# A fused two-layer attention kernel: the preparation stage is dissolved into the start of the key side

## The chip, the cores and the metric

The kernel runs on one core of one Trainium2 chip. The metric is the device time of one execution in microseconds, the median of three runs. A core has TensorE (PE: matmuls and transpositions, results in PSUM), VectorE (DVE), ScalarE (ACT), GpSimd (POOL) and SyncE (SP), which here issues DMAs. Each engine works through its own list of instructions in order; semaphores hold an engine until another has got far enough.

## The reference

Two layers work on `x` (32 batches, 64 rows, 512 columns) with a context of the same shape. Layer 0 is an attention with eight heads and a feed forward with ternary weights. Layer 1 is a linear attention and a gated low-rank projection. The parts that matter here:

```python
# layer 0 attention: 64x64 weights and biases
q = _proj(Wq, bq, x_query); k = _proj(Wk, bk, x_key); v = _proj(Wv, bv, x_value)
...
return _proj(Wo, bo, x)
# layer 1 attention: Wq, Wk, Wv are 512x64, Wo is 64x512
kh = jnp.einsum('bcn,oc->bon', k, Wk).reshape(b, HEADS, DIM_HEAD, -1)
vh = jnp.einsum('bcn,oc->bon', v, Wv).reshape(b, HEADS, DIM_HEAD, -1)
kh = jax.nn.softmax(kh, axis=-1)
context = jnp.einsum('bhdn,bhen->bhde', kh, vh)
out = jnp.einsum('bhde,bhdn->bhen', context, qh)
out = jnp.einsum('bcn,oc->bon', out, Wo) + bo[None, :, None]
```

`kh` and `vh` of layer 1 come from the context input alone. So the kernel computes the product of keys and context for all batches first, with `Wv` and `Wo` of each head multiplied into one matrix, and keeps it as `M`.

## The kernel before

The program is a chain of blocks, in the order of `program`: `prepare`, `key_side`, `attention0`, `feed_forward`, `query_side`, `projection`, `experts`. All engines meet at the end of each block, so nothing of a block starts before the one ahead of it is finished on every engine.

`prepare` makes what later blocks need of small weights and constants. SP loads the key weights of layer 1 twice side by side (`wdup`, so that both halves of the partitions hold them), the first context tile (`cf0`), `wv1` and `wo1`, the query weights, the second context tile and the first three pieces of the feed forward's weights. ScalarE issues 14 loads: two biases, four 64x64 weights in two copies, and `bv`, `bo` in two copies. Then it loads its table of functions. TensorE turns (transposes) the key weights into PSUM. ScalarE copies them in half precision (`wk_hi`) and DVE subtracts this copy (`wk_lo`), so that two halves carry the accuracy of one float. The same is done with the query weights. `Wo1` is turned and copied (`wo1T`), multiplied with `wv1` head by head, and scaled into `wv_wo`. The four small weights are turned and copied into `wT0` for layer 0. The biases are split into three rows of short floats (`biases`).

`key_side` works on 16 tiles of 128 rows (two batches each), four chunks of 128 key columns to a tile. For each tile GpSimd makes `cs_hi` (`high`) and DVE `cs_lo` (`low`) from `cf`. For each chunk TensorE makes the keys in one of two PSUM buffers (`keys`, six matmuls), DVE takes the maximum of a row (`keys_max`), and ScalarE two exponentials with their sums (`exponentials`). With all four chunks of a tile done, TensorE turns them back (`turn`, into `psT`), ScalarE and DVE copy them (`eT`), TensorE multiplies them with the turned context (`gather`, into `psG`) and with `wv_wo` (`matrix`, into `psM`), and DVE writes `M`. TensorE is written one tile ahead: it makes the keys of tile t+1 between the turns of tile t, so five keys groups (tile 0 and the first chunk of tile 1) stand before the loop. This start is the "ramp" below.

Beside this the weights of the feed forward pass twice through a ring of three buffers. In tiles 0 to 6 they are summed (`magnitudes`), then DVE makes `winv` (`scales`), and from tile 7 on GpSimd rounds them (`ternary`) and SP sends them through transposing DMAs (`turn` on SP). SP's loads wait for counts of tiles or of sums. The order of each engine is the order in which the code issues; no scheduler changes it.

## Time and profile before

| | us |
|---|---|
| median of 3 runs | 810.43 (809.3 to 810.54) |
| the profiled execution | 810.15 |
| its span in the profile | 808.3 |
| TensorE busy | 687.0 (85%) |
| VectorE busy | 621.2 (77%) |
| ScalarE busy | 483.1 (60%) |
| GpSimd busy | 364.2 (45%) |

The busy shares are means over stages with different limits. The preparation stage lies in the first 19 us; the key side goes on to about 233 us. A row of the timeline gives the start, the duration, the engine, the line of the kernel, the operation with what it writes and reads, and how many of its kind are merged in it. In square brackets stands how long the engine had been idle before it, and what released it. "issue" there is time in which the engine waited for nothing that the profile shows. SPq and ACTq are the issuing of DMAs by SP and ScalarE. The granted clock is the share of TensorE's full 2.4 GHz.

### The profile page before, as it was taken

The numbers are of one execution on the slowest core, as the hardware profiler recorded it, in microseconds if no ns is written. First come the engines' busy times: TensorE is split into PE (matmuls) and PEld (weight loads), VectorE is DVE, ScalarE is ACT, GpSimd is POOL, SyncE is SP. The second block draws the span as 40 slices with busy tenths as digits, with TensorE's granted clock in tenths as the row PEclk, the third lists the DMA queues.
The fourth block names the chain that finished last, engine by engine and source line by source line (L and its number), as shares of the span: only waits on it lengthen the run. The fifth ranks groups of instructions, "written<-read, shape, count | busy, mean of one in ns | idle before, by whom it ended". The sixth has DMA issues, their size and how long they took to land. (4 is left out here: it accounts for less than half of the span.)

```text
span 808.3 us, 17679 instructions
## 1 busy us (share of the span) xinstructions
PE 687.0 (85%) x6606; PEld 357.8 (44%) x6633; DVE 621.2 (77%) x1028; ACT 483.1 (60%) x873; POOL 364.2 (45%) x271
## 2 busy tenths in 40 slices
PE   2799999999977767499999479999999999479944
PEld 1345454554545555244444134444444444145541
DVE  4687788888636667499998579999999999355456
ACT  1687867667525657277777247787878787422100
POOL 1000008999925664022212146767777776343100
PEclk9999999999999999599999969999999999879955
DMA  5043555555442331023343100000000000035305
GB/s 149 27 136 111 200 186 147 157 147 154 89 126 77 72 82 30 15 56 74 74 71 70 37 0 1 2 2 0 2 1 2 2 1 1 1 72 85 53 2 208
DMA packets 94504, 54.98 MB, mean 68 GB/s; under 512 B 78868, under 2 KB 78868, under 8 KB 94420
## 3 DMA queue, kind: packets, MB, share of 16 engines
q1 hardware_dynamic: 93456, 53.71, 26.5%
q8 instruction: 54, 0.88, 0.4%
q10 hardware_dynamic: 964, 0.13, 0.1%
q14 instruction: 30, 0.25, 0.1%
HBM read 32.27 MB, written 4.19 MB: 45 GB/s over the span
## 5 line engine op out<-in xcount | busy, mean ns | idle before, releaser
L1314 POOL TENSOR_TENSOR query_qn<-query_eq,query_rq 128x1024 f32<-128x1024 f32 x64 | 121.7, 1902 | 56.6 <-DVE query_rq L1248 54.7
L610 ACT ACTIVATE keys_ek<-keys_psK,keys_mk 128x512 f32<-128x512 f32 x128 | 86.8, 684 | 39.8 <-DVE keys_mk L524 38.1
L524 DVE TENSOR_REDUCE keys_mk<-keys_psK 128x2 f32<-128x1024 f32 x64 | 77.9, 1217 | 22.5 <-PE keys_psK L662 21.7
L1239 DVE TENSOR_REDUCE query_mq<-query_psQ 128x16 bf16<-128x1024 f32 x64 | 75.6, 1181 | 5.0 <-PE query_psQ L1382 4.8
L1245 DVE TENSOR_REDUCE query_lq<-query_eq 128x16 f32<-128x1024 f32 x64 | 77.2, 1207 | 2.6 <-ACT query_eq L1323 2.5
L1323 ACT ACTIVATE query_eq<-query_psQ 128x1024 f32<-128x1024 f32 x64 | 65.2, 1018 | 22.6 <-PE query_psQ L1395 22.6
L1404 PE MATMUL query_psX<-all_ident,query_qn 128*128 128x128 f32 x512 | 70.4, 281 | 0.0
L673 PE MATMUL keys_psT<-all_ident,keys_ek 128*128 128x128 f32 x512 | 70.1, 280 | 0.0
L685 PE MATMUL keys_psG<-keys_eT,keys_cT 128*64 128x512 f32 x256 | 69.0, 617 | 1.0 <-issue 0.9
L1042 POOL TENSOR_SCALAR ff_hr<-ff_h,ff_qs 128x1376 f32<-128x1376 f32 x16 | 22.6, 1412 | 104.5 <-DVE ff_qs L1089 104.5
L673 PEld LDWEIGHTS keys_psT<-all_ident,keys_ek 128*128 128x128 f32 x512 | 54.8, 141 | 27.9 <-issue 21.3
L1330 ACT ACTIVATE query_qT<-query_psX 128x1024 f32<-128x1024 f32 x64 | 65.4, 1022 | 0.9 <-PE query_psX L1404 0.9
L1414 PE MATMUL query_psF<-query_qT,all_M 128*64 128x512 f32 x256 | 61.8, 604 | 1.1 <-ACT query_qT L1330 1.1
L1404 PEld LDWEIGHTS query_psX<-all_ident,query_qn 128*128 128x128 f32 x512 | 55.3, 142 | 15.7 <-issue 14.3
L499 POOL TENSOR_SCALAR keys_st<-all_ring 128x1024 bf16<-128x1024 f32 (+2 forms) x16 | 60.7, 3795 | 1.3
L487 POOL TENSOR_SCALAR keys_cs_hi<-all_cf 128x512 f16<-128x512 f32 x16 | 9.9, 618 | 106.8 <-DMA all_cf<-in_ctx_dram 82.4
L529 DVE COPY keys_eT<-keys_psT 128x512 f32<-128x512 f32 x80 | 53.1, 680 | 2.6 <-PE keys_psT L673 2.3
L1163 PE MATMUL ff_psG<-all_wgT,ff_xT 128*128 128x512 bf16 (+1 forms) x190 | 45.9, 364 | 10.1 <-DMA ff_xT<-ff_xq 10.1
L1136 ACT ACTIVATE ff_r<-ff_psG,all_sg 128x512 f32<-128x512 f32 (+1 forms) x48 | 30.8, 642 | 35.7 <-PE ff_psG L1163 34.0
L1537 PE MATMUL proj_psH<-all_ring,proj_x_T 128*128 128x512 f16 x192 | 46.1, 392 | 0.0
L1177 PE MATMUL ff_psD<-all_wdT,ff_hT 128*128 128x512 bf16 (+1 forms) x171 | 39.6, 379 | 7.0 <-DMA ff_hT<-ff_hq 6.8
L1168 PE MATMUL ff_psU<-all_wuT,ff_xT 128*128 128x512 bf16 (+1 forms) x188 | 45.0, 362 | 0.2
(243 smaller groups left out, 1436.3 us busy)
## 6 DMA issues: line engine op xcount, KB each, us to landing
all_ring<-in_L_ffn_w_down_dram SPq DMA_DIRECT2D x8, 688.0 KB, 4.3
all_ring<-in_L_ffn_w_gate_dram SPq DMA_DIRECT2D x10, 512.0 KB, 6.6
all_ring<-in_L_ffn_w_up_dram SPq DMA_DIRECT2D x10, 512.0 KB, 3.7
all_cf<-in_ctx_dram SPq DMA_DIRECT2D x16, 256.0 KB, 2.7
all_x_res<-in_x_dram SPq DMA_DIRECT2D x4, 1024.0 KB, 6.2
att_ctx_n<-in_ctx_dram SPq DMA_DIRECT2D x16, 256.0 KB, 3.2
out_dram<-all_x_res SPq DMA_DIRECT2D x16, 256.0 KB, 2.2
att_w_nat<-in_L_ffn_W_dram SPq DMA_DIRECT2D x4, 256.0 KB, 4.2
```

The source lines that it names most:

```text
L499: pool.tensor_scalar(st[v % 2][:, 0:w], r, -ROUND, 0.0, ALU.add, ALU.add).then_inc(cast_ok, 1)
L524: dve.tensor_reduce(mk[:, c, :], psK[c % 2][:, :, :], X, ALU.max, negate=True).then_inc(mk_ok, 1)
L610: act.activation(ek[t % 2][b][:, c, :], psK[c % 2][:, b, :], ACT.Exp, bias=mk[:, c, b:b + 1], accum_out=le[t % 2][:, b, c:c + 1]).then_inc ...
L673: mm = pe.transpose(chunk(psT[b], c), chunk(ek[t % 2][b][:, c, :], j), k.ident[:, :])
L685: mm = pe.matmul(psG[HALF[b], :], cT[t % 2][:, j, b * D:(b + 1) * D], eT[b][:, j, :], start=j == 0, stop=j == NC - 1)
L1239: dve.tensor_reduce(mq[g % 2][:, :, 0:HEADS], psQ[g % 2][:, :, :].rearrange("p b (h d) -> p b h d", d=D), X, ALU.max, negate=True).then_in ...
L1245: dve.tensor_reduce(lq[:, :], eq[g % 3][:, :, :], X, ALU.add).then_inc(lq_ok, 1)
L1314: pool.tensor_tensor(qn[m % 2][:, :, :], eq[m % 3][:, :, :], rq[m % 2][:, :].unsqueeze(2).broadcast_to([P, 2 * HEADS, D]), ALU.mult).then_ ...
L1323: act.activation(eq[g % 3][:, :, :].rearrange("p h d -> p (h d)"), psQ[g % 2][:, :, :].rearrange("p b n -> p (b n)"), ACT.Exp).then_inc(eq ...
L1330: act.activation(qT[t % 2][:, :, c * P:(c + 1) * P], psX[:, :, :].rearrange("p b (j n) -> p (b j) n", n=P), ACT.Copy).then_inc(qT_ok, 1)
L1404: mm = pe.transpose(psX[:, b, j * P:(j + 1) * P], qn[g % 2][:, b * HEADS + 2 * j:b * HEADS + 2 * j + 2, :].rearrange("p h d -> p (h d)"), ...
L1414: mm = pe.matmul(psF[HALF[b], :], k.M[:, 2 * t + b, j, :], qT[t % 2][:, b * NC + j, :], start=j == 0, stop=j == NC - 1)
```

## The change

`prepare` and its block are gone. Its work is written into the lists of `key_side`, with a semaphore where there was a barrier.

- Loads. ScalarE issues only `cf0`, `wv1` and `wo1` and loads its table. SP issues the key weights, `cf1`, the four small weights (once each), the query weights, the biases and the first ring pieces. `bv` and `bo` are loaded by SP at tile 2.
- TensorE turns the key weights and `Wo1`, then makes the keys of chunks 0 and 1. The small weights, the query weights and the product of `wv1` and `wo1T` follow between the next keys groups.
- DVE makes `wk_lo` and both `cs_lo`, and then, between the maxima of tile 0, `wq_hi` (before on ScalarE), `wq_lo`, `wT0` (before on ScalarE) and `wv_wo`. The biases follow in three portions in tiles 1 to 3.
- Buffers. `wdup` lies in `eT1`; the PSUM results lie in `psT0`, `psT1` and `psG`, which are free until the first turn. The other small buffers belong to the key side.

```diff
+        wdup = eT[1][:, 0:2, :].rearrange("p m (c d) -> p m c d", c=NC)
...
@@ key_side, SP
+            for h in range(2):
+                sp.dma_start(wdup[:, 1, :, h * D:(h + 1) * D], a["Wk1"].rearrange("(c p) d -> p c d", p=P)).then_inc(wk_in, 16)
+            sp.dma_start(cf[1][:, :], nat[1]).then_inc(c_in[1], 16)
+            for n, w in enumerate((a["Wq0"], a["Wk0"], a["Wv0"], a["Wo0"])):
+                sp.dma_start(w_two[:, n, :], w).then_inc(two_in, 16)
+            for h in range(2):
+                sp.dma_start(wdup[:, 0, :, h * D:(h + 1) * D], a["Wq1"].rearrange("(c p) d -> p c d", p=P)).then_inc(wq_in, 16)
...
+                if t == 2:
+                    for h in range(2):
+                        sp.dma_start(k.bv2[HALF[h], :], a["bv0"].unsqueeze(1)).then_inc(two_in, 16)
+                        sp.dma_start(k.bo2[HALF[h], :], a["bo0"].unsqueeze(1)).then_inc(two_in, 16)
@@ key_side, VectorE
+            dve.wait_ge(wkhi_ok, 1)
+            dve.tensor_tensor(k.wk_lo[:, :], psT[0][:, :], k.wk_hi[:, :], ALU.subtract).then_inc(w_ok, 1)
             low(0)
+            dve.wait_ge(w_ps, O_TURNED)
+            dve.tensor_copy(wo1T[:, :, :], psG[:, 0:NC * D].rearrange("p (n m) -> p n m", n=NC)).then_inc(w_ok, 1)
             low(1)
-            for c in range(NC + 1):
-                keys_max(c // NC, c % NC)
...
             for t in range(TILES + 1):
...
+                    if c == 0 and 1 <= t < 4:
+                        biases(t - 1)
@@ key_side, ScalarE
+            act.dma_start(cf[0][:, :], nat[0]).then_inc(c_in[0], 16)
+            act.dma_start(wv1[:, :, :], a["Wv1"].rearrange("(c p) d -> p c d", p=P)).then_inc(vo_in, 16)
+            act.dma_start(wo1[:, :], a["Wo1"]).then_inc(vo_in, 16)
+            act.preload_act_table_set("natural_log_exp_and_others")
+            act.wait_ge(w_ps, K_TURNED)
+            act.activation(k.wk_hi[:, :], psT[0][:, :], ACT.Copy).then_inc(wkhi_ok, 1)
+            act.wait_ge(const_ok, CONSTS)
@@ key_side, TensorE
+            turned_keys()
+            turned_output()
+            pe.wait_ge(w_ok, WK_OK)
+            keys(0, 0)
+            keys(0, 1)
+            context(0)
+            turned_two()
+            turned_queries()
+            keys(0, 2)
+            product()
+            keys(0, 3)
+            pe.wait_ge(const_ok, CONSTS)
+            keys(1, 0)
+            pe.wait_ge(w_ok, VO_OK)
@@ program
-                    prepare(nc, a, k)
                     key_side(nc, a, k)
```

What the change moves on VectorE, at the start of the program. Before, its list runs from the first use of the turned key weights (`wk_lo`) through the whole preparation to the first maxima:

```order
L229 TENSOR_TENSOR all_wk_lo<-prep_psK,all_wk_hi 128x512 [waits prep_hi_ok]
L231 COPY prep_wo1T<-prep_psO 128x256 [waits prep_t_ps]
L233 TENSOR_TENSOR all_wq_lo<-prep_psQ,all_wq_hi 128x512 [waits prep_hi_ok]
L202 CAST prep_part<-prep_brow 1x128 [waits all_b_in]
...
L239 TENSOR_SCALAR all_wv_wo<-prep_psV 64x4x64 [waits prep_zero_ok,prep_t_ps]
L239 TENSOR_SCALAR all_wv_wo<-prep_psV 64x4x64 x3
L120 UNCONDITIONAL_BRANCH
L514 UNCONDITIONAL_BRANCH [waits barrier_Pool_Activation_PE_DVE_SP_release]
L519 TENSOR_TENSOR keys_cs_lo<-all_cf,keys_cs_hi 128x512 [waits keys_hi_ok] x2
L524 TENSOR_REDUCE keys_mk<-keys_psK 128x2 [waits keys_k_ps] x4
```

In the changed kernel the same engine has, from `wk_lo` on:

```order
L492 TENSOR_TENSOR all_wk_lo<-keys_psT,all_wk_hi 128x512 [waits keys_wkhi_ok]
L406 TENSOR_TENSOR keys_cs_lo<-all_cf,keys_cs_hi 128x512 [waits keys_hi_ok]
L495 COPY keys_wo1T<-keys_psG 128x256 [waits keys_w_ps]
L406 TENSOR_TENSOR keys_cs_lo<-all_cf,keys_cs_hi 128x512 [waits keys_hi_ok]
L411 TENSOR_REDUCE keys_mk<-keys_psK 128x2 [waits keys_k_ps] x2
L500 CAST all_wq_hi<-keys_psT 128x512 [waits keys_w_ps]
L502 TENSOR_TENSOR all_wq_lo<-keys_psT,all_wq_hi 128x512 [waits keys_wkhi_ok]
L411 TENSOR_REDUCE keys_mk<-keys_psK 128x2 [waits keys_k_ps]
L505 COPY all_wT<-keys_psT 64x256 x2
L411 TENSOR_REDUCE keys_mk<-keys_psK 128x2 [waits keys_k_ps]
L511 TENSOR_SCALAR all_wv_wo<-keys_psG 64x4x64 [waits keys_zero_ok,keys_w_ps]
```

The maxima (`keys_mk`) stood behind all of the preparation; now query weights, small weights and product stand between them, and the bias instructions are no longer here.

On TensorE, before, the five parts of the preparation stand ahead of the block's end and of the first keys:

```order
L248 MATMUL prep_psK<-all_ident,prep_wdup 128x128 [waits prep_k_in,prep_ident_ok]
...
L252 MATMUL prep_psO<-all_ident,prep_wo 128x64 [waits prep_vo_in]
...
L256 MATMUL prep_psQ<-all_ident,prep_wdup 128x128 [waits prep_q_in]
...
L260 MATMUL prep_psW<-all_ident,prep_w_two 64x128 [waits prep_two_in]
...
L265 MATMUL prep_psV<-prep_wo1T,prep_wv 64x64 [waits prep_oT_ok]
...
L645 UNCONDITIONAL_BRANCH [waits barrier_Pool_Activation_PE_DVE_SP_release]
L662 MATMUL keys_psK<-keys_cs_hi,all_wk_hi 128x512 [waits keys_lo_ok]
```

Now TensorE's list begins so; `keys_w_two` are the small weights, `keys_eT` holds the key and later the query weights:

```order
L657 MATMUL keys_psT<-all_ident,keys_eT 128x128 [waits keys_wk_in,keys_ident_ok]
...
L663 MATMUL keys_psG<-all_ident,keys_wo 128x64 [waits keys_vo_in]
...
L617 MATMUL keys_psK<-keys_cs_hi,all_wk_hi 128x512 [waits keys_lo_ok,keys_w_ok]
...
L617 MATMUL keys_psK<-keys_cs_hi,all_wk_hi 128x512 [waits keys_lo_ok]
...
L669 MATMUL keys_psT<-all_ident,keys_w_two 64x64 [waits keys_two_in]
...
L675 MATMUL keys_psT<-all_ident,keys_eT 128x128 [waits keys_wq_in]
...
L617 MATMUL keys_psK<-keys_cs_hi,all_wk_hi 128x512 [waits keys_ek_ok,keys_lo_ok]
...
L682 MATMUL keys_psG<-keys_wo1T,keys_wv 64x64 [waits keys_w_ok]
```

Two parts are left ahead of the first keys; the small weights and the query weights stand behind the second keys group, and the product behind the third.

## Rows read from the trace of the kernel before

**Rows 1.** Busy time of each engine in two stretches, granted clock, DMA share, GB/s

```profile
10.00:20.00 10.00, 2.11 (x20) 1.47 (x20) 5.30 (x18) 2.81 (x5) 0.66 (x2) 1.00 0.31 111
140.00:160.00 20.00, 20.00 (x151) 10.18 (x149) 17.30 (x26) 12.45 (x31) 19.50 (x13) 1.00 0.54 141
```

**Rows 2.** Timeline to 21 us: start, duration, engine, line, operation, count, idle before

```profile
0.72 1.00 SPq L142 DMA_DIRECT2D prep_wdup<-in_L_xattn_Wk_dram  x2
...
4.44 1.09 PE L248 MATMUL prep_psK<-all_ident,prep_wdup 128*128 128x128 f32 x4 [4.44 <-DMA prep_wdup<-in_L_xattn_Wk_dram]
...
6.95 0.69 PE L252 MATMUL prep_psO<-all_ident,prep_wo 64*128 64x64 f32 x4 [1.42 <-DMA prep_wo<-in_L_xattn_Wo_dram]
...
7.99 1.12 PE L256 MATMUL prep_psQ<-all_ident,prep_wdup 128*128 128x128 f32 x4 [0.36 <-DMA prep_wdup<-in_L_xattn_Wq_dram]
...
9.69 1.28 ACT L163 ACT_TABLE_LOAD   x1 [9.69 <-issue]
10.98 0.60 ACT L165 ACTIVATE all_wk_hi<-prep_psK 128x512 f16<-128x512 f32 x1
...
11.61 0.69 DVE L229 TENSOR_TENSOR all_wk_lo<-prep_psK,all_wk_hi 128x512 f16<-128x512 f32 x1 [7.23 <-ACT all_wk_hi L165]
...
13.15 0.20 DVE L202 CAST prep_part<-prep_brow 1x128 bf16<-1x128 f32 x1
...
14.92 0.49 DVE L209 CAST all_bias_rows<-prep_rest 1x256 bf16<-1x256 f32 x2
...
15.02 1.06 PE L260 MATMUL prep_psW<-all_ident,prep_w_two 128*64 128x128 f32 x4 [5.91 <-DMA all_bo<-in_L_xattn_bo_dram]
...
17.18 1.76 DVE L239 TENSOR_SCALAR all_wv_wo<-prep_psV 64x256 f32<-64x256 f32 x4 [1.77 <-PE prep_psV L265]
19.34 1.20 POOL L487 TENSOR_SCALAR keys_cs_hi<-all_cf 128x512 f16<-128x512 f32 x2 [15.92 <-POOLq L120]
...
21.14 0.61 PE L662 MATMUL keys_psK<-keys_cs_hi,all_wk_hi 64*128 64x512 f16 x2 [4.01 <-DVE keys_cs_lo L519]
```

**Rows 3.** Groups by line and shape up to 19.3 us, VectorE: busy, mean ns, idle

```profile
L231 DVE COPY prep_wo1T<-prep_psO 128x256 f32<-128x256 f32 x1 | 0.4, 411 | 0.0
```

**Rows 4.** Busy time in the third microsecond, columns as rows 1

```profile
2.00:3.00 1.00, 0.00 (x0) 0.00 (x0) 0.44 (x1) 0.00 (x0) 1.00 (x2) 1.00 0.95 211
```

**Rows 5.** Groups by line from 24 to 34 us, VectorE

```profile
L524 DVE TENSOR_REDUCE keys_mk<-keys_psK 128x2 f32<-128x1024 f32 x5 | 6.1, 1224 | 4.0 <-PE keys_psK L662 3.2 <-ACT keys_ek L610 0.8
```

**Rows 6.** Timeline of the ramp, ScalarE's exponentials

```profile
23.90 0.69 ACT L610 ACTIVATE keys_ek<-keys_psK,keys_mk 128x512 f32<-128x512 f32 x1 [7.01 <-DVE keys_mk L524]
...
25.15 0.20 ACT L610 ACTIVATION_READ_ACCUMULATOR keys_ek<-keys_psK,keys_mk 128x1 f32 x1
...
31.96 0.69 ACT L610 ACTIVATE keys_ek<-keys_psK,keys_mk 128x512 f32<-128x512 f32 x1 [0.22 <-DVE keys_mk L524]
```

**Rows 7.** Busy time in two stretches of the ramp

```profile
26.00:28.00 2.00, 0.79 (x8) 0.25 (x6) 1.23 (x1) 1.77 (x5) 0.00 (x0) 0.88 0.00 0
28.00:30.00 2.00, 1.79 (x10) 0.43 (x8) 0.97 (x1) 1.54 (x5) 0.62 (x1) 0.50 0.00 0
```

**Rows 8.** Busy time over one tile of the steady key side

```profile
40.00:52.60 12.60, 12.41 (x92) 6.34 (x88) 9.62 (x12) 10.99 (x28) 1.24 (x2) 1.00 0.39 122
```

**Rows 9.** Timeline of SP in the third tile

```profile
49.19 0.36 SPq L431 DMA_DIRECT2D all_cf<-in_ctx_dram  x1
...
61.78 0.34 SPq L431 DMA_DIRECT2D all_cf<-in_ctx_dram  x1
66.27 4.66 SPq L299 DMA_DIRECT2D all_ring<-in_L_ffn_w_up_dram  x3
```

**Rows 10.** Timeline at the end of the key side

```profile
224.90 1.26 SPq L455 DMA_TRANSPOSE all_wdT<-keys_st  x1
```

**Rows 11.** Waits of SP: total, times, longest

```profile
SPq L480 <- DMA all_wdT<-keys_st: 3.2, 1, 3.2
```

More of the change, by code:

```diff
@@ L478, in _ @@
                         again(v + RING)
+            sp.wait_ge(two_in, 16 * 8)
             sp.wait_ge(turn_in[0], turned_by(UNITS - 2))
@@ new lines, in _ @@
+            keys_max(0, 2)
+            for h in range(2):
+                dve.tensor_copy(k.wT0[HALF[h], :, :], psT[0][0:D, 0:4 * D].rearrange("p (n m) -> p n m", n=4)).then_inc(w_ok, 1)
+            keys_max(0, 3)
+            dve.wait_ge(w_ps, PRODUCT)
+            dve.wait_ge(zero_ok, 3)
+            for r, bank in enumerate((psG, psT[1])):
+                for b, rows in enumerate(HALF):
+                    dve.tensor_scalar(k.wv_wo[rows, r:HEADS:2, b * D:(b + 1) * D],
+                                      bank[0:D, :].rearrange("p (h m) -> p h m", h=HEADS)[:, r:HEADS:2, :],
+                                      D ** -0.5, None, ALU.mult).then_inc(w_ok, 1)
@@ L569, in _ @@
+            keys_max(1, 0)
             for t in range(TILES + 1):
@@ L696, in matrix, with turned_keys, turned_output, turned_two @@
                 mm.then_inc(m_ps, 1)
-            for c in range(NC + 1):
-                keys(c // NC, c % NC)
-                if c == 0:
-                    context(0)
+            def turned_keys():
+                pe.wait_ge(ident_ok, 1)
+                pe.wait_ge(wk_in, 16 * 2)
+                for c in range(NC):
+                    mm = pe.transpose(chunk(psT[0], c), wdup[:, 1, c, :], k.ident[:, :])
+                mm.then_inc(w_ps, 1)
+            def turned_output():
+                pe.wait_ge(vo_in, 16 * 2)
+                for c in range(NC):
+                    mm = pe.transpose(psG[:, c * D:(c + 1) * D], chunk(wo1, c), k.ident[0:D, 0:D])
+                mm.then_inc(w_ps, 1)
+            def turned_two():
+                pe.wait_ge(two_in, 16 * 4)
+                for n in range(4):
+                    mm = pe.transpose(psT[0][0:D, n * D:(n + 1) * D], w_two[:, n, :], k.ident[0:D, 0:D])
+                mm.then_inc(w_ps, 1)
+            def turned_queries():
+                pe.wait_ge(wq_in, 16 * 2)
+                for c in range(NC):
+                    mm = pe.transpose(chunk(psT[1], c), wdup[:, 0, c, :], k.ident[:, :])
+                mm.then_inc(w_ps, 1)
+            def product():
+                pe.wait_ge(w_ok, WQ_OK)
+                for h in range(HEADS):
+                    r = HALF[h % 2]
+                    mm = pe.matmul((psG, psT[1])[h % 2][0:D, h * D:(h + 1) * D], wv1[r, h // 2, :], wo1T[r, h // 2, :],
+                                   start=True, stop=True)
+                mm.then_inc(w_ps, 1)
+            turned_keys()
[12 more added lines that the diff above has]
+            pe.wait_ge(w_ok, VO_OK)
             for t in range(TILES + 1):
```

201 lines of the change are left out of this document (66 added, 135 removed).

## The prediction

> **What bounds the kernel now.** I began with the busy time of the engines in equal stretches [rows 1]. In the key side proper, from 140 to 160 us, TensorE is busy for all of the 20 us. In the stretch from 10 to 20 us it is busy for 2.11 of 10. So the kernel begins with a phase that no engine fills, and then comes a long one that TensorE bounds. The second view is the timeline of the first 21 us [rows 2], which says what this phase waits for. The key weights are turned on TensorE at 4.44 us, but their high part `wk_hi` is copied only at 10.98 us: ScalarE issues 14 small loads one after the other and then the table of functions (9.69 us), and only then comes to it. TensorE turns the four small weights at 15.02 us, since it waits for the last of those loads. The weight product ends in four DVE scalings at 17.18 us. GpSimd sat idle for 15.92 us before the first `cs_hi`, for the end of the block. The first matmul of the key side starts at 21.14 us. Everything in the key side counts from there: its loads, casts and transposes wait for counts of tiles, none for a clock on the wall.
>
> The ends of the key side are in [rows 10, 11]. The last `M` on DVE runs from 232.04 to 232.73 us. The last transposing DMA is issued at 224.90 us for 1.26 us, and SP waits 3.2 us for it, so this stream ends near 229.4 us, 3.3 us before the other. The stream of casts on GpSimd that feeds it waits for `winv` from DVE, which the code places in the eighth tile, so it moves with the tiles.
>
> **The change part by part.** All sums are made against the profiled execution, 810.15 us (span 808.3 us and 1.85 around it). The median of the plain runs is 810.43 us, 0.03% away.
>
> *Start of the first key matmul.* The chain that is left is: key weights in, turned, `wk_hi`, `wk_lo`, `cs_lo` of tile 0, matmul. In [rows 2] the weights are in at 4.44 us. ScalarE has three loads instead of 14 ahead of the table. Half a microsecond each from 0.72 us and 1.28 us for the table give about 3.6 us, so the table is ready before the weights are turned. With turning 1.09, `wk_hi` 0.60, `wk_lo` 0.69, `cs_lo` 0.69 (the same kind and shape as `wk_lo`) and 0.1 of handing over, the matmul would start at 7.6 us. That is the early end. GpSimd is no part of it: it needs `cf0` and 0.6 us for `cs_hi` (two took 1.20), and has the time of turning and of `wk_hi` for it.
>
> Two transfers can hold this back. `cf0` (256 KB) is now issued at 0.72 us from ScalarE, beside the key weights, and in the third microsecond the DMA engines are busy for 0.95 of the time at 211 GB/s [rows 4]. 256 KB at this rate are 1.2 us. Part of them had also moved before the weights were in, so I take 0.5 us between 0 and 1.2. And TensorE now turns `Wo1` ahead of the first keys, so it waits for `wo1` and `wv1`. Before, `wo1` was in at 6.95 us with 768 KB (key weights, `cf0`, `wv1`, `wo1`) issued up to it; now `cf1` is issued ahead as well. I take 7.4 us for it, between 6.9 and 8.0, and 0.69 for its four transposes: 8.1 us. Both chains give 8.1 to 8.2, and I take 8.3 us for the first key matmul (7.6 to 9.0). **Term 1: 21.14 - 8.3 = 12.8 us gained** (12.1 to 13.5).
>
> The Trainium skill bears on the first of the two. Its page "DMA: Bandwidth & Descriptors", section "Issuing engines are not separate DMA queues", says that loads issued by ScalarE and SP run on the same 16 engines and interleave. It speaks against this change: taken at its hardest, the issues spread over two engines save issue time alone, the whole 1.2 us is paid and the gain is 0.7 us less than my sum. With two independent paths it would be 0.5 more. The busy share of 0.95 fits the rule.
>
> *The ramp.* Up to the first exponentials of tile 1 the engines take turns: matmuls into one of two PSUM buffers, maximum on DVE (1.22 us), two exponentials on ScalarE (from 23.90 to 25.35 us for the first pair, 1.45), next matmul [rows 5, 6]. The change puts on DVE, in this stretch: `wo1T` 0.41, `wq_hi` (was on ScalarE) and `wq_lo` 0.69 each like `wk_lo`, `wT0` twice 0.41 (the price of `wo1T` [rows 3], a copy from PSUM as large on each partition), `wv_wo` 1.76 [rows 2], 4.4 us together. DVE sat idle for 4.0 us between 24 and 34 us [rows 5], so it isn't clear that it pays. I laid the order out by hand from 8.3 us. `wo1T` fits before the first maximum (9.8 us). Maxima 0 and 1 end at 12.5. `wq_hi` and `wq_lo` run from 12.9 to 14.3, where maximum 2 would have started near 13.7. The product needs `wq_lo`, so keys 3 start at 15.1. `wT0` ends at 16.4 and maximum 3 at 17.6; `wv_wo` runs to 19.4, maximum 0 of tile 1 to 20.65, and its exponentials start at 20.7. Before they started at 31.96, 10.8 us after the first key matmul; now 12.4. **Term 2: 1.6 us lost.** The other ends are nothing (all in DVE's idle time) and 4.4 (all on the path). TensorE's added work (turning the queries 1.12 and the small weights 1.06 us at most [rows 2], a product of 16 short matmuls of about that price) lies in its own waits: each keys group there waits longer for ScalarE or for `wq_lo`.
>
> *Biases.* Their ten DVE instructions take 2.3 us in a row, from 13.15 to 15.41 [rows 2], and now stand in three portions of 0.5 to 0.9 us in tiles 1 to 3. A tile takes 12.6 us there (from one load of context at 49.19 to the next at 61.78 us [rows 9]), of which TensorE is busy 12.41 us and DVE 9.62 [rows 8]: 3 us a tile cover 0.9. **Term 3: 0.3 us lost**, between 0 and 2.3 (all portions falling where TensorE waits for `eT`).
>
> *Loads on SP.* SP issues eleven loads before the weights of the feed forward instead of eight: six small ones have come over from ScalarE, and `cf0`, `wv1` and `wo1` have gone to it. The query weights are issued by about 6 us; before, they were issued by 4.8 and in at 7.99, so now they are in near 9.5, needed at 12.3. The first ring loads come some 2 us later than before and are not used before the ramp is over. The next context tile is asked for after the first transposition of context, now moved behind two keys groups, at 11.9 us, and used ten later. Four bias loads stand at tile 2 ahead of the ring loads, some 3 us of SP. There SP issues `cf` at 61.78 and the next ring load at 66.27 [rows 9], a wait of 4.1 us that covers them; uncovered they would cost the difference in one tile, under 3 us. I take nothing.
>
> *Blocks.* The barrier between the blocks (last `wv_wo` ends 18.94, GpSimd starts 19.34) is in term 1.
>
> Sum: 12.8 - 1.6 - 0.3 = 10.9 us gained, **799.2 us**. The end follows since both streams of [rows 10, 11] count from tiles.
>
> **The clock.** The granted clock was 0.50, the 1.2 GHz level, from 28 to 30 us, after stretches in which TensorE was mostly idle (0.79 us of the two before 28 us [rows 7]), and 1.00 in the full stretches of [rows 1, 8]. In my ramp TensorE has more to do between keys, and where it is slower DVE is later still, so this changes no term.
> The Trainium skill's page "TensorE: Matmul & The Clock Gate", section "What's actually happening", says that the half rate is the resting state and that sustained work releases it. By that rule the half rate can't last in the full stretch, and rival 4 has a low chance; the trace agrees, with 1.00 in both stretches.
>
> **The rivals.**
> 1. *DVE's chain takes it all.* The weights' work is serial with maxima and exponentials, and the bias portions with the `eT` copies. For it: ScalarE waits for DVE's maxima in the ramp. Against it: 4.0 us of idle DVE. Gain 12.8 - 4.4 - 2.3 = 6.1, 804.1 us. Chance 0.12.
> 2. *The loads crowd each other.* The key weights come in only when all that was in at 7.99 us before is in (that is when the query weights were turned, [rows 2]). First matmul at 7.99 + 1.09 + 0.60 + 0.69 + 0.69 + 0.1 = 11.2; gain 9.9 - 1.9 = 8.0, 802.1 us. For it: the busy share; against it: the key weights stand first in SP's queue. Chance 0.10.
> 3. *Casts and transposes set the end.* If their stream didn't move, the end could come only 3.3 us earlier: 806.9 us. For it: GpSimd is busy for 19.50 of the 20 us from 140 us on [rows 1]. Against it: its start waits for `winv`. Chance 0.03.
> 4. *Slower:* the half clock of 28 to 30 us moves into the stretch that TensorE bounds and stays. One tile at half rate costs 12.4 us more of TensorE, so it decides from about one tile on; a tile and a half give 799.2 + 18.6 = 817.8 us. Chance 0.04.
> 5. *It doesn't do what it says:* a wait that I overlooked (for the small weights or the constants) holds the keys until 20 us; about 810 us. Chance 0.03.
>
> My own course has the remaining 0.68. A measurement of this kernel can tell about 0.2% (1.6 us) from no change. Faster: 0.68 + 0.12 + 0.10 + 0.03 = 0.93; same 0.03; slower 0.04. The range: early loads and a ramp half hidden give 799.2 - 0.7 - 0.9 = 797.6; upwards it takes in rival 2 and nearly rival 1: 803.8.
>
> **What would show it.** In the profile after: the first psK matmul between 7.6 and 9.0 us; `wk_hi` right behind the turned key weights, not behind a load; first exponentials of tile 1 near 20.7; DVE without long waits between 13 and 20 us; no new wait of TensorE in tiles 1 to 3; the end of the last `M` near 222 and the stages behind it as long as before. I am wrong if the first exponentials of tile 1 come after 25 us, if a tile in the steady stretch lasts over 12.6 us, or if a stage behind the key side grows.

## The result, and the profile of the changed kernel

| | before | changed |
|---|---|---|
| median, us | 810.14 (809.3 to 810.54, 4 runs) | 799.92 (799.79 to 800.49, 4 runs) |
| profiled execution, us | 810.15 | 799.84 |
| its span, us | 808.3 | 797.8 |
| last `M` of the key side, us | 232.04 | 222.22 |

The ratio is 0.9874, with a 95% interval of 0.986 to 0.9887. The forecast was 799.2 us, in a range of 797.6 to 803.8. The time is right, but not every term of it: the first is 1.3 us too large, the third charges 0.3 us for what cost nothing, and 0.6 us came where nothing was forecast.

The first view is the timeline of the changed kernel up to the first keys, columns as in [rows 2].

```profile
2.24 1.28 ACT L573 ACT_TABLE_LOAD   x1 [2.24 <-issue]
...
4.09 0.62 POOL L364 TENSOR_SCALAR keys_cs_hi<-all_cf 128x512 f16<-128x512 f32 x1 [0.67 <-DMA all_cf<-in_ctx_dram]
...
6.42 1.09 PE L657 MATMUL keys_psT<-all_ident,keys_eT 128*128 128x128 f32 x4 [6.42 <-DMA keys_eT<-in_L_xattn_Wk_dram]
...
7.43 0.69 PE L663 MATMUL keys_psG<-all_ident,keys_wo 64*128 64x64 f32 x4
...
8.78 0.68 DVE L406 TENSOR_TENSOR keys_cs_lo<-all_cf,keys_cs_hi 128x512 f16<-128x512 f32 x1
```

The key weights are turned at 6.42 us; before it was 4.44 [rows 2]. The table was loaded by 3.52 us and the first context tile was in by 4.09, so both wait for the weights. From there the chain is as it was laid out: `wk_hi` and `wk_lo` follow at once, and `cs_lo` ends at 9.46 (8.78 + 0.68).

The second is TensorE in the ramp.

```profile
9.60 0.61 PE L617 MATMUL keys_psK<-keys_cs_hi,all_wk_hi 64*128 64x512 f16 x2 [1.48 <-DVE keys_cs_lo L406]
...
10.41 0.65 PE L617 MATMUL keys_psK<-keys_cs_hi,all_wk_lo 64*128 64x512 f16 x2
...
14.80 0.38 PE L617 MATMUL keys_psK<-keys_cs_hi,all_wk_lo 64*128 64x512 f16 x2
...
20.76 0.61 PE L617 MATMUL keys_psK<-keys_cs_hi,all_wk_hi 64*128 64x512 f16 x2 [1.31 <-DVE all_wv_wo L511]
...
22.16 1.88 PE L628 MATMUL keys_psT<-all_ident,keys_ek 128*128 128x128 f32 x8
...
24.73 1.10 PE L628 MATMUL keys_psT<-all_ident,keys_ek 128*128 128x128 f32 x8
```

The first key matmul starts at 9.60 us. A pair of key matmuls lasts 0.61 to 0.65 us at first, 0.38 from 14 us on, and 0.61 again at 20.76; the eight turns at 22.16 last 1.88 us, and the next eight 1.10. This slow stretch at 20 us is called the dip below. The third view is the granted clock and the busy time, columns as in [rows 1].

```profile
8.00:12.00 4.00, 2.52 (x14) 0.84 (x12) 3.12 (x5) 0.14 (x1) 0.74 (x3) 1.00 1.05 325
10.00:20.00 10.00, 7.44 (x58) 3.38 (x54) 8.22 (x12) 5.65 (x16) 0.62 (x1) 1.00 0.39 139
20.00:24.00 4.00, 3.24 (x16) 1.88 (x18) 3.13 (x4) 2.52 (x8) 0.00 (x0) 0.57 0.00 0
130.00:150.00 20.00, 20.00 (x152) 10.49 (x152) 17.32 (x25) 12.54 (x31) 19.50 (x13) 1.00 0.54 130
```

Between 10 and 20 us TensorE now works 7.44 us, against 2.11 in [rows 1], and the full stretch (130 to 150 us here) is as before. The granted clock is 0.57 from 20 to 24 us, where pairs and turns are slow; it is 1.00 from 8 to 12 us, where the pairs last 0.65 as well. The next two fences are ScalarE, to compare with [rows 6], and VectorE.

```profile
22.00 0.69 ACT L558 ACTIVATE keys_ek<-keys_psK,keys_mk 128x512 f32<-128x512 f32 x1 [1.48 <-DVE keys_mk L411]
```
```profile
14.46 0.69 DVE L500 CAST all_wq_hi<-keys_psT 128x512 f16<-128x512 f32 x1 [0.85 <-PE keys_psT L675]
...
19.84 0.86 DVE L511 TENSOR_SCALAR all_wv_wo<-keys_psT 64x256 f32<-64x256 f32 x2
20.74 1.23 DVE L411 TENSOR_REDUCE keys_mk<-keys_psK 128x2 f32<-128x1024 f32 x1
```

The first exponentials of tile 1 come at 22.00 us, 12.40 after the first key matmul. VectorE has one wait of note between 13 and 20 us, 0.85 us for the turned queries. Last, SP in the steady part and the end of the key side, to compare with [rows 9 to 11].

```profile
39.49 0.34 SPq L292 DMA_DIRECT2D all_cf<-in_ctx_dram  x1
...
52.10 0.34 SPq L292 DMA_DIRECT2D all_cf<-in_ctx_dram  x1
...
54.27 0.60 SPq L340 DMA_DIRECT2D all_bo<-in_L_xattn_bo_dram  x1
56.58 0.37 SPq L147 DMA_DIRECT2D all_ring<-in_L_ffn_w_up_dram  x1
```
```profile
222.22 0.69 DVE L426 TENSOR_TENSOR all_M<-keys_psM,keys_rl 128x512 f32<-128x512 f32 x1 [3.04 <-PE keys_psM L649]
```
```profile
SPq L357 <- DMA all_wdT<-keys_st: 2.1, 1, 2.1
```

The load at 49.19 in [rows 9] is the one at 39.49 here, and 61.78 is 52.10: 9.70 and 9.68 us earlier. The last `M` is 9.82 us earlier. SP waits 2.1 us for the last transposition in place of 3.2 [rows 11].

### The profile page after: what moved, and what is told of

Read it like the earlier page. It is cut to its first block and busy times, and to the rows that moved or that the text cites. A ratio compares the mean times of both kernels' runs of the same rounds, so it can differ in the third digit from the quotient of the medians.

```text
span 797.8 us, 17690 instructions
## 1 busy us (share of the span) xinstructions
PE 691.3 (87%) x6633; PEld 358.0 (45%) x6633; DVE 622.4 (78%) x1031; ACT 482.2 (60%) x870; POOL 364.8 (46%) x271
## 5 line engine op out<-in xcount | busy, mean ns | idle before, releaser
L1175 PE MATMUL ff_psD<-all_wdT,ff_hT 128*128 128x512 bf16 (+1 forms) x176 | 42.1, 389 | 4.1 <-DMA ff_hT<-ff_hq 4.1
```

## The experiments

I read three marks in each trace: the first key matmul, the load of context that is at 49.19 us in [rows 9], and the last `M`. The ramp is the time from the first mark to the second. From the second to the last `M` it is 182.71 to 182.73 us in all eleven versions of the changed kernel, and 182.85 to 182.88 in the three of the kernel before. So what a version gains in the key side is decided ahead of the second mark. Marks are those of one traced execution. Each ratio compares a run with the kernel before on the same chip, and the medians come from several chips, so ratios say more than medians. Behind the last `M`, where the code is the same in all fourteen kernels, the traced executions took from 575.1 to 580.8 us; so a few microseconds between two single executions are no evidence, and the marks carry most of what follows.

In the text the runs go by these names without the number.

| run | key weights turned | first key matmul | context load | ramp | last `M` | median | ratio (95%) |
|---|---|---|---|---|---|---|---|
| before | 4.44 | 21.14 | 49.19 | 28.05 | 232.04 | 810.14 | |
| changed | 6.42 | 9.60 | 39.49 | 29.89 | 222.22 | 799.92 | 0.9874 (0.986 to 0.9887) |
| e1_scalar_loads_late | 5.95 | 9.14 | 38.37 | 29.23 | 221.09 | 800.84 | 0.9857 (0.9837 to 0.9877) |
| e2_keys_on_both | 3.78 | 7.55 | 38.43 | 30.88 | 221.15 | 799.94 | 0.985 (0.9826 to 0.9874) |
| e9_output_turned_later | 3.88 | 7.07 | 37.62 | 30.55 | 220.34 | 797.76 | 0.9851 (0.9823 to 0.988) |
| e10_early_filler | 3.88 | 7.07 | 35.30 | 28.23 | 218.03 | 795.66 | 0.9828 (0.98 to 0.9856) |
| e12_scalings_split | 3.89 | 7.08 | 34.47 | 27.39 | 217.19 | 795.15 | 0.9812 (0.9795 to 0.9829) |
| e7_filler | 6.01 | 9.20 | 39.27 | 30.07 | 222.00 | 800.38 | 0.9869 (0.9839 to 0.9899) |
| e5_scalings_twice | 6.01 | 9.21 | 41.80 | 32.59 | 224.52 | 803.11 | 0.9906 (0.9879 to 0.9933) |
| e3_maxima_first | 6.61 | 9.80 | 41.93 | 32.13 | 224.65 | 803.13 | 0.9884 (0.9861 to 0.9907) |
| e8_keys_first_maxima_first | 3.70 | 8.00 | 41.20 | 33.20 | 223.92 | 802.11 | 0.9888 (0.9862 to 0.9915) |
| e6_biases_at_once | 6.23 | 9.41 | 39.48 | 30.07 | 222.19 | 802.17 | 0.9888 (0.9852 to 0.9923) |
| e4_before_bias_loads_late | 4.15 | 17.85 | 48.68 | 30.83 | 231.54 | 808.23 | 0.9945 (0.9928 to 0.9963) |
| e11_before_late_loads_filler | 4.30 | 16.88 | 43.55 | 26.67 | 226.43 | 804.14 | 0.9928 (0.9904 to 0.9952) |

**What held the key weights.** Two runs on the loads. The first moves ScalarE's table ahead of its loads.

```diff
+            act.preload_act_table_set("natural_log_exp_and_others")
             act.dma_start(cf[0][:, :], nat[0]).then_inc(c_in[0], 16)
             act.dma_start(wv1...); act.dma_start(wo1...)
-            act.preload_act_table_set("natural_log_exp_and_others")
```

> The changed kernel, with ScalarE's three loads (context tile 0, wv1, wo1) issued behind its table load, so about 1.3 us later. In the changed kernel the key weights were in at 6.42 us (4.44 before). Theory A (the three loads from ScalarE share the DMA engines with the key weights and delay them): key weights in at 5.2 us or earlier. But wo1 is issued later too and TensorE turns it ahead of the first keys, so the first key matmul comes between 8.8 and 9.8 us and the time stays within 1 us of 799.9. Rival B (the key weights come late for another reason, the destination or the loads behind them on SP): in at 6.4 us as before, first key matmul at 9.6 or, with wo1 later, up to 10.5 us; time 799.9 to 800.9.

```profile
0.71 1.28 ACT L570 ACT_TABLE_LOAD   x1 [0.71 <-PEq L1784]
...
0.74 0.42 ACTq L571 DMA_DIRECT2D all_cf<-in_ctx_dram  x1
...
5.95 1.09 PE L657 MATMUL keys_psT<-all_ident,keys_eT 128*128 128x128 f32 x4 [5.95 <-DMA keys_eT<-in_L_xattn_Wk_dram]
```

The edit did not do what I wanted: ScalarE issued the load of `cf0` at 0.74 us, beside its table (0.71 to 1.99). So the loads were not late, the weights came 0.47 us earlier, which may be the scatter between executions (5.95 to 6.61 in the six runs with these loads), and the run says nothing on the cause. The second run issues one half of the key weights from each engine, and `cf0` from SP behind them.

```diff
-            for h in range(2):
-                sp.dma_start(wdup[:, 1, :, h * D:(h + 1) * D], ...).then_inc(wk_in, 16)
+            sp.dma_start(wdup[:, 1, :, 0:D], ...).then_inc(wk_in, 16)
+            sp.dma_start(cf[0][:, :], nat[0]).then_inc(c_in[0], 16)
...
-            act.dma_start(cf[0][:, :], nat[0]).then_inc(c_in[0], 16)
+            act.dma_start(wdup[:, 1, :, D:P], ...).then_inc(wk_in, 16)
```

> The changed kernel, with the two copies of the key weights issued at the same moment from SP and from ScalarE, and context tile 0 moved to SP behind them, so that nothing but key weights is at the head of either queue. Theory A (sharing of the DMA engines): key weights in at 4.5 us or earlier, first key matmul near 7.5 us (then bound by wo1 and its turning), gain on the changed kernel about 2 us: 797.9. Rival B (late for another reason): in at 6 us or later, 799.9 unchanged.

```profile
3.78 1.09 PE L657 MATMUL keys_psT<-all_ident,keys_eT 128*128 128x128 f32 x4 [3.78 <-DMA keys_eT<-in_L_xattn_Wk_dram]
...
5.11 0.62 POOL L364 TENSOR_SCALAR keys_cs_hi<-all_cf 128x512 f16<-128x512 f32 x1 [1.69 <-DMA all_cf<-in_ctx_dram]
...
7.38 0.47 PE L663 MATMUL keys_psG<-all_ident,keys_wo 64*128 64x64 f32 x2 [2.51 <-DMA keys_wo<-in_L_xattn_Wo_dram]
```

The weights are in at 3.78 us and `cf0` now comes after them (5.11). In the changed kernel `cf0`, issued at the same moment from the other engine, came first (4.09) and the weights 2.3 us later. The new buffer of the weights is the same in both, so it is not the cause. What moved beside the weights can be read from the bytes, first in the changed kernel and then in the one before, columns as in [rows 1].

```profile
0.00:6.42 6.42, 0.00 (x1) 0.03 (x1) 2.69 (x13) 1.28 (x1) 3.28 (x10) 1.00 0.80 154
0.00:4.44 4.44, 0.00 (x0) 0.03 (x1) 2.72 (x13) 0.00 (x0) 2.65 (x9) 1.00 0.53 126
```

Until the weights were used, 0.99 MB had moved in the changed kernel (6.42 us at 154 GB/s) and 0.56 MB before. The 0.43 MB more are 2.0 us at the 211 GB/s of [rows 4], which is what the weights lost. They are more than the 256 KB of `cf0`, so other loads moved ahead of the last weights too. The run made two changes at once, splitting the weights over two engines and putting `cf0` behind them; which of the two brings how much isn't separated. The start moved by 2.05 us only as far as `wo1` let it (TensorE waited 2.51 us for it until 7.38), and the last `M` by 1.07: the ramp became a microsecond longer. Whether any of the expected 2 us is in the time can't be told, since the interval of this run overlaps that of the changed kernel. The next pair shows why the ramp grew. The Trainium skill's page "DMA: Bandwidth & Descriptors", section "Issuing engines are not separate DMA queues", says that loads issued by several engines interleave on the same DMA engines; the changed kernel agrees, where the key weights of SP came 1.98 us later beside the loads of ScalarE.

**What the ramp is made of.** The kernel before, with the four loads of `bv` and `bo` issued behind `wq_hi`.

```diff
-            for h in range(2):
-                act.dma_start(k.bv2[HALF[h], :], ...).then_inc(two_in, 16)
-                act.dma_start(k.bo2[HALF[h], :], ...).then_inc(two_in, 16)
...
             act.activation(k.wq_hi[:, :], psQ[:, :], ACT.Copy).then_inc(hi_ok, 1)
+            for h in range(2):
+                act.dma_start(k.bv2[HALF[h], :], ...).then_inc(bo_in, 16)
+                act.dma_start(k.bo2[HALF[h], :], ...).then_inc(bo_in, 16)
```

> The kernel before, with the preparation stage kept as it is, but ScalarE's last four loads (bv and bo) issued behind its wq_hi copy and waited for by themselves, so that TensorE turns the small weights as soon as these are in. Theory E (most of the preparation's length was the order of loads on ScalarE, not the barrier): small weights turned near 10 us in place of 15, first key matmul near 17.5 us, 3 to 4 us of the gain without merging the stages: 806.5. Rival F (the barrier and the serial chain hold it): first key matmul still after 20 us, 809 or more.

```profile
17.85 0.61 PE L661 MATMUL keys_psK<-keys_cs_hi,all_wk_hi 64*128 64x512 f16 x2 [4.00 <-DVE keys_cs_lo L518]
...
29.00 0.61 PE L661 MATMUL keys_psK<-keys_cs_hi,all_wk_hi 64*128 64x512 f16 x2 [0.97 <-ACT keys_ek L609]
...
30.39 1.97 PE L672 MATMUL keys_psT<-all_ident,keys_ek 128*128 128x128 f32 x8
...
36.53 0.39 PE L661 MATMUL keys_psK<-keys_cs_hi,all_wk_hi 64*128 64x512 f16 x2
```
```profile
18.00:34.00 16.00, 13.15 (x56) 4.68 (x53) 8.75 (x10) 9.65 (x26) 0.62 (x1) 1.00 0.05 17
```

The keys start 3.29 us earlier, so this much of the 11.54 us needs no merging of the stages, only four loads out of the way. But the context load comes only 0.51 us earlier. From 17.85 to 34 us every pair of key matmuls lasts 0.61 to 0.66 us, and eight turns 1.97; later they last 0.39 and 1.09. Successive pairs start 0.40 and 0.43 us apart there (17.85, 18.25, 18.68) and 0.22 later (36.53, 36.76, 36.98). These are the durations of the dip in the changed kernel, where the granted clock was 0.57, and of the stretches at 1.00 behind it. So I take the first for the lower level of the clock, 1.2 GHz, and the second for the upper, 2.4, although the column of the granted clock says 1.00 in all of it. In this ramp TensorE waited 0.45 to 0.98 us before the third to the sixth group of keys. Then the same kernel with transpositions of the identity into unused PSUM: 8 behind the product, 6 ahead of the keys, and

```diff
             for c in range(NC + 1):
                 keys(c // NC, c % NC)
                 if c == 0:
                     context(0)
+                elif c < NC:
+                    filler(5)
```

> The kernel before with bv and bo loaded later (as in the run before_bias_loads_late: first key matmul 3.3 us earlier, but the context load near 49 only 0.5 us earlier) and filler transpositions: 8 behind the product, 6 ahead of the first keys, 5 behind each of keys (0,1), (0,2), (0,3). Theory: the 2.8 us were lost because TensorE stayed at the slow durations (0.61 to 0.66 for a keys pair, 1.97 for eight turns) from 17.9 to 34 us, for want of work before; with filler the durations are 0.38 and 1.09 from 20 us on and the ramp is 28.0 to 28.6 long from the first key matmul to the context load near 46: 2 to 2.8 us earlier than 48.68, last M at 228.8 to 229.6. Rival: the 2.8 us went to DMA or VectorE; then filler leaves the context load at 48.7 or later.

```profile
16.88 0.39 PE L663 MATMUL keys_psK<-keys_cs_hi,all_wk_hi 64*128 64x512 f16 x2 [1.03 <-DVE keys_cs_lo L520]
...
26.89 1.09 PE L674 MATMUL keys_psT<-all_ident,keys_ek 128*128 128x128 f32 x8
```
```profile
26.43 0.69 ACT L611 ACTIVATE keys_ek<-keys_psK,keys_mk 128x512 f32<-128x512 f32 x1 [0.44 <-DVE keys_mk L525]
```

With more work the ramp was 4.16 us shorter (30.83 to 26.67), and 1.38 shorter than in the kernel before; I had expected 28.0 at the least. The code of the two ramps differs by the filler alone, and their durations by the level of TensorE's clock. The device times do not follow the marks. The ratio of the first of the two runs is worth 4.5 us, though its last `M` came only 0.50 us earlier than that of the kernel before; and the ratios of the two runs differ by 1.4 us, with overlapping intervals, where their last `M` differ by 5.11. In the second, the profiled execution took 801.56 us, and the five others 803.96 to 806.44. Whether TensorE was at the upper level in those can't be told, since one execution is traced. So 4.16 us is the difference of two executions, not a measured gain in time.

The changed kernel, with filler in two places of its ramp only:

```diff
+            filler(8)
             keys(1, 0)
+            filler(6)
             pe.wait_ge(w_ok, VO_OK)
```

> The changed kernel with 14 transpositions of the identity into psT0 on TensorE in the two waits of the ramp before and behind the first keys group of tile 1; their result is overwritten. In the changed kernel the granted clock falls to the 1.2 GHz level about 20.7 to 24 us, right where the first eight turns run (1.88 us, 1.09 at full rate). Theory I (the half rate delays the third keys group of tile 1 and what follows by about 0.3 us): with the waits filled the clock stays at 1.00, turns take 1.1 us, the steady tiles come 0.2 to 0.8 us earlier. Rival J: the filler itself comes in the way, or the clock falls in any case; nothing gained or up to 1 us lost.

The dip at 20 us is gone (the first eight turns take 1.09 us), which doesn't show that the filler did it: it is absent without filler in scalar_loads_late, biases_at_once and output_turned_later too. And the keys start 0.40 us earlier and the last `M` comes only 0.22 earlier. TensorE was at the lower level until 15.3 us in this execution and until 13.8 in that of the changed kernel, although their instructions are the same up to there; this takes back what the missing dip gives. So the next two runs take `wo1` off the start (with the loads of keys_on_both), and then fill from the beginning.

```diff
-            turned_output()
             pe.wait_ge(w_ok, WK_OK)
             keys(0, 0)
             keys(0, 1)
+            turned_output()
```

> Changed kernel with the halves of the key weights issued from SP and ScalarE (as in the run keys_on_both) and, in addition, Wo1 turned behind the second keys group instead of ahead of the first, its copy wo1T behind the second maximum. In the run keys_on_both TensorE waited 2.51 us for wo1 and the first key matmul came at 7.55, although cs_lo was ready near 6.8. My theory: wo1 sets the start there, so the first key matmul comes at 6.9 to 7.0, 0.6 us earlier; the ramp behind it is as long as there (30.9 from the first key matmul to the context load near 38.4) since TensorE is at the slow durations (0.61 to 0.66 for a pair) until 16, so the last M comes 0 to 0.6 us earlier than 221.15. Rival: the start is not what counts, the transfers of the query weights and the product are; then the last M stays at 221.1.

The first key matmul comes at 7.07 us, 0.48 earlier than in keys_on_both, and the last `M` 0.81 earlier, of which 0.39 are the dip that this execution didn't have (from the first exponentials of tile 1 to the context load it takes 17.12 us, in keys_on_both 17.51). Then the filler:

```diff
+            early(6)
             turned_keys()
+            early(7)
             pe.wait_ge(w_ok, WK_OK)
             keys(0, 0)
...
```

> The same kernel with filler: transpositions of the identity on TensorE (6 ahead of the key weights, 7 between the key weights and the first keys, 8 behind keys (0,3), 6 behind keys (1,0)), which add work and take nothing away. Theory: TensorE's slow durations until 16 us and again at 20 come from its idle time before; with work from 2 us on the keys pairs last 0.38 from about 8 us on, not 0.61 to 0.66. Of the 1.6 us that the slow durations cost from the first key matmul on (6 groups of keys, turns) about 1 us comes back, less 0 to 0.6 us where a filler stands in the way: last M 219.8 to 220.8. Rival: the ramp is set by VectorE's chain alone, and filler changes nothing (last M within 0.2 us of the run without it). Second rival: filler only delays: last M 0.5 us later.

```profile
7.07 0.39 PE L617 MATMUL keys_psK<-keys_cs_hi,all_wk_hi 64*128 64x512 f16 x2 [0.72 <-DVE keys_cs_lo L406]
...
17.71 1.09 PE L628 MATMUL keys_psT<-all_ident,keys_ek 128*128 128x128 f32 x8
```
```profile
18.20 0.69 ACT L558 ACTIVATE keys_ek<-keys_psK,keys_mk 128x512 f32<-128x512 f32 x1 [1.47 <-DVE keys_mk L411]
```

The pairs last 0.39 us from the first one on, and the last `M` comes 2.31 us earlier than without filler, more than the 1 us that I expected. The medians of the two runs, taken on the same chip, are 2.10 us apart (797.76 and 795.66). And the level is no accident here: all nine traced executions of the changed kernel's versions without early filler begin their keys at 0.60 us or more for a pair, and the two with it are at 0.39 from the first (early_filler) or the third pair on (scalings_split). The ramps of both kernels can now be compared at the upper level: from the first key matmul to the first exponentials of tile 1 it is 11.13 us here (18.20 - 7.07) and 9.55 in before_late_loads_filler (26.43 - 16.88): 1.58 us. To the context load it is 28.23 against 26.67: 1.56. This is the cost of the change in the ramp with the clock taken out, but for `Wo1`, which is turned inside the ramp here.

**Is the weights' work on VectorE serial?** One run doubles the four scalings (1.72 us) into a buffer that nothing reads.

```diff
+            for r, bank in enumerate((psG, psT[1])):
+                for b, rows in enumerate(HALF):
+                    dve.tensor_scalar(twin[rows, r:HEADS:2, :], ...).then_inc(w_ok, 1)
             keys_max(1, 0)
```

> The changed kernel with the four scalings of wv_wo (1.72 us on VectorE) done a second time into a spare buffer, in the same place behind the fourth maximum. Theory C (VectorE is the path of the ramp there): everything from the first maximum of tile 1 on comes 1.7 us later, 801.6. Rival (idle time of VectorE covers it): less than 0.5 us, 799.9 to 800.4.

```profile
22.27 0.61 PE L623 MATMUL keys_psK<-keys_cs_hi,all_wk_hi 64*128 64x512 f16 x2 [3.09 <-DVE keys_twin L517]
...
23.66 1.97 PE L634 MATMUL keys_psT<-all_ident,keys_ek 128*128 128x128 f32 x8
```

The ramp is 2.70 us longer than in the changed kernel. The first exponentials of tile 1 come at 23.50, 1.89 us later from the first key matmul, so the 1.72 us are paid in full; and TensorE, which waited 3.09 us for VectorE, is at the lower level from 22.3 to 27 us. Two runs put the maxima first and let three of the four scalings run inside tile 0; on TensorE the product moves behind the fourth keys group:

```diff
-            keys_max(1, 0)
+            scaled(0, 0)
             for t in range(TILES + 1):
...
+                    if c == 0 and t == 0:
+                        scaled(0, 1)
+                        scaled(1, 0)
+                        scaled(1, 1)
```

> The changed kernel with the same work in another order: on VectorE the maxima of the ramp stand ahead of wq_lo, wT0 and the scalings of wv_wo (three of these behind the second maximum of tile 1), on TensorE the product stands behind the fourth keys group, and the waits for wT0 and wv_wo stand right ahead of the first turns that overwrite their PSUM. Theory C (the 1.6 us lost in the ramp are DVE work that stands in front of maxima): first exponentials of tile 1 about 20 us in place of 22.0, and the steady tiles 0.5 to 1.6 us earlier: 798.3 to 799.4. Rival D (the work has to be done before the first turns anyway, whatever the order): exponentials earlier but the turns wait for wv_wo, steady tiles as in the changed kernel or later: 799.9 or more.

```profile
21.33 0.66 PE L636 MATMUL keys_psT<-all_ident,keys_ek 128*128 128x128 f32 x4
24.25 0.66 PE L636 MATMUL keys_psT<-all_ident,keys_ek 128*128 128x128 f32 x4 [2.27 <-DVE all_wv_wo L501]
...
26.03 1.97 PE L636 MATMUL keys_psT<-all_ident,keys_ek 128*128 128x128 f32 x8
```

The exponentials of tile 1 did come earlier (20.86 us), but the turns into `psT1`, where half of the product lies, waited 2.27 us for the scalings, and then TensorE was at the lower level (1.97 us for eight turns). With the earlier weights it is the same:

> Both changes together: key weights at the head of both queues, and the maxima of the ramp ahead of the other work of VectorE. If the gains of the two single changes are independent: about 2 us for the loads and 0.5 to 1.6 for the order, 796.3 to 797.4. If the order is worth nothing: 797.9. If the loads are worth nothing either: 799.9.

The last `M` is at 223.92 us, 2.77 later than in keys_on_both, which has the same loads. What was wrong was which scalings were late. The last run leaves those of `psT1` where they are, and moves the two of `psG` behind the first `eT` copy; TensorE waits for each pair where it needs it.

```diff
+            scaled(1)
             keys_max(1, 0)
...
                         turned(t, c, 1)
+                    if c == 0 and t == 0:
+                        scaled(0)
```

> The kernel of the run early_filler, in which at full rate of TensorE the ramp was 28.2 us long (first key matmul 7.07, context load 35.30) against 26.7 in before_late_loads_filler. Here two of the four scalings into wv_wo (0.86 us) move behind the first eT copies of tile 0, so the maximum of tile 1 starts before them, and TensorE waits for the scalings ahead of the turn and the product that need them, not ahead of keys (1,1). Theory: VectorE's work on the weights is serial with the maxima in the ramp, and this is what is left of the 1.6 us of term 2. So the first exponentials of tile 1 come 0.9 us earlier (18.20 to 17.3), the context load 0.5 to 0.9 us earlier (34.4 to 34.8). Rival: the two scalings then hold the first products of tile 0, as all of them did in the run maxima_first (there the context load came 2.4 us later); the context load is at 35.3 or later.

```profile
15.22 0.86 DVE L511 TENSOR_SCALAR all_wv_wo<-keys_psT 64x256 f32<-64x256 f32 x2
16.10 1.23 DVE L411 TENSOR_REDUCE keys_mk<-keys_psK 128x2 f32<-128x1024 f32 x1
...
19.53 0.85 DVE L511 TENSOR_SCALAR all_wv_wo<-keys_psG 64x256 f32<-64x256 f32 x2
```

The first exponentials of tile 1 come at 17.36 us and the context load at 34.47, 0.83 us earlier: the time of the two scalings (0.85). This version is 0.9812 of the kernel before, and its interval lies below that of the changed kernel, so it is the faster of the two, though they were not run side by side. In time it can't be told from early_filler, whose interval overlaps its own.

**The biases.** All ten instructions in one piece in tile 1:

```diff
-                    if c == 0 and 1 <= t < 4:
-                        biases(t - 1)
+                    if c == 0 and t == 1:
+                        for n in range(3):
+                            biases(n)
```

> The changed kernel with all three portions of the bias work in one piece in tile 1 (2.3 us on VectorE in a row). The portions of 0.5 to 0.8 us cost nothing between tiles 1 and 4. Theory G (VectorE has about 3 us to spare in a tile, and each copy of eT about 1 us before TensorE needs it): a piece of 2.3 us overruns the slack of one slot and costs 0.3 to 1.3 us once. Rival H (the slack of the whole tile counts): 0.0.

```profile
36.28 0.16 DVE L455 CAST keys_part<-keys_brow 1x128 bf16<-1x128 f32 x1
...
38.01 0.49 DVE L447 CAST all_bias_rows<-keys_rest 1x256 bf16<-1x256 f32 x2
```
```profile
39.48 0.34 SPq L292 DMA_DIRECT2D all_cf<-in_ctx_dram  x1
...
52.08 0.34 SPq L292 DMA_DIRECT2D all_cf<-in_ctx_dram  x1
```

They hold VectorE for 2.2 us in a row (36.28 to 38.50). The keys groups of TensorE on both sides of the piece start at 35.70 and 39.33 us, and in the changed kernel at 35.71 and 39.35; the next tile takes 12.60 us (52.08 - 39.48), there 12.61. So they cost nothing. The median of this run (802.17) is above what its marks say; its four executions spread from 799.43 to 804.52.

## Why the prediction was right, by its own steps

**Term 1 was too large: 11.54 us in place of 12.8**, outside its bounds of 12.1 to 13.5. The step that failed is the first transfer that "can hold this back": I took 0.5 us for `cf0` beside the key weights, at most 1.2 (its bytes at the rate of [rows 4]), and it was 1.98 (6.42 - 4.44). The bound counted the bytes of `cf0` alone, and 0.43 MB more than before moved until the weights were used, 2.0 us at that rate. The rest of the term was right: from the weights to the first matmul it took 3.18 us (9.60 - 6.42) where 3.17 were laid out, and `wo1`, forecast for 7.4 us, was turned at 7.43, right behind the key weights, so it was in by then at the latest.

**Term 2 was right: 1.58 us in place of 1.6** up to the first exponentials of tile 1 (12.40 against 10.82). The order laid out by hand holds too: with the 1.3 us of the later start added, `wv_wo` was to end at 20.7 us and the maximum of tile 1 at 21.95, and they end at 20.70 and 21.97. scalings_twice and scalings_split show that this is VectorE's serial work: 1.72 us of scalings more put these exponentials 1.89 us later (23.50 - 9.21 against 12.40), and 0.86 less put them 0.85 earlier (17.36 - 7.08 against 11.13). That the size fits to the hundredth is luck: the same order took 12.13 us in scalar_loads_late, where TensorE's durations fell to 0.39 at 13.6 us, and 12.96 in biases_at_once, where they fell at 15.5. To the context load the ramp is 1.84 us longer. The other 0.26 are the dip: from these exponentials to the context load it takes 17.49 us here, 17.23 before, and 17.10 to 17.12 in the seven traces without a dip.

**Term 3 was 0.0 in place of 0.3.** The context loads keep their distance (52.10 - 39.49 against 61.78 - 49.19), and biases_at_once costs nothing either. The loads of `bv` and `bo` (52.48 to 54.87 us) end ahead of the next ring load at 56.58, which the prediction took at nothing.

**The sum.** 11.54 - 1.84 + 0.13 (the steady part) = 9.83 us up to the last `M`. Of the 10.31 us between the profiled executions 0.49 are left behind the key side; there the feed forward waited 4.1 us for `ff_hT` where it had waited 7.0, in stages whose code is the same. That is scatter between executions, as far as I can see, and no part of the change; behind the last `M` the traced executions differ by up to 5.7 us. The forecast of 10.9 is 0.6 above 10.31: -1.26 of term 1, -0.24 of term 2, +0.3 of term 3 and +0.62 of what I took at nothing. The time came out closer than its largest term, and that is luck: the errors cancel, and the 0.49 us could as well have been two.

**The clock.** "This changes no term" came true for the difference and was wrong as a picture of the ramp. Both ramps contain the lower level: it cost about 1.38 us before (28.05 - 26.67) and 1.66 after (29.89 - 28.23; the two versions compared here also load the weights and turn `Wo1` in another order). They nearly cancel. Had only one ramp been slow, as in before_bias_loads_late, the sum would have been off by up to 4 us (4.16 in that pair of traces). I had read the granted clock alone [rows 7], and not the durations in [rows 2], where the first pair of key matmuls lasts 0.61 us.

**The rivals.** 1, VectorE serial: true of the ramp in mechanism, but it had priced all 4.4 us of added work, and 1.6 came. 2, crowding loads: half true, 1.98 us of the 3.55 it needed (7.99 - 4.44). 3, casts and transposes: no. The last transposing DMA is issued at 215.33 us for 1.40 us, and SP waits 2.1 for it, so this stream ends near 218.8 in place of 229.4 and moved with the tiles. 4, the half clock: it lasted from 20.76 to 24 us and did not enter the steady stretch; scalings_twice shows it to 27 us, and before_bias_loads_late to 34. 5, an overlooked wait: no, the keys start at 9.60 us.

## What to carry to other kernels

Ask of a load on which a chain hangs what else is issued in the same half microsecond from any engine: count all the bytes that can move beside it, not those of the nearest load. Splitting the urgent load over two issuing engines, with the large load behind it, gave the 2 us back with 0.66 us more. In a start-up phase of short turns between engines, read TensorE's durations against those of the steady stretch; if they are double, dummy work ahead of and in its waits can pay (2.3 us here). When work moves into a phase where one engine is the chain, it costs its full time, unless it is put where that engine waits; and what holds a buffer that the next engine needs must not be the part that is put off.

## What the hardware did that I had not expected

- By its durations TensorE ran at the lower level for 16 us (before_bias_loads_late, 17.85 to 34) with waits of 0.45 to 0.98 us between groups of keys, while the granted clock read 1.00: 0.61 to 0.66 against 0.38 us for a pair of 512-column matmuls, 1.97 against 1.09 for eight transpositions.
- With 27 dummy transpositions (early_filler) the ramp was 2.3 us shorter, and with 29 (before_late_loads_filler) 4.2, each between two traced executions; the medians moved by 2.1 us in the first case and can't tell in the second.
- The same instructions changed level at 13.8 us in one execution (changed) and at 15.3 in another (filler). The dip at 20 us came in changed and keys_on_both, and not in scalar_loads_late, biases_at_once and output_turned_later.
- ScalarE issued DMAs during its table load (0.74 to 2.22 us beside 0.71 to 1.99).
- Of two loads issued together at 0.72 us from two engines, 256 KB of context in long rows were used at 4.09 us and 256 KB of weights in rows of 256 bytes at 6.42. 0.99 MB had moved by then. Whether the length of the rows, the queue or the two issues of the weights decides this was not tried.
